# Moving the output stores from SyncE to ScalarE's DMA queue, one group of four images later

## What is computed

```
xa_n = inorm(xa)                                     # each image by its own mean and variance
k, q = spec_conv(xa_n, kw, (64, 64)), spec_conv(xa_n, qw, (64, 64))
v    = spec_conv(xa_n, vw, (256, 256))               # only 8 x 8 low frequencies are kept
att  = softmax(q @ k.T * sqrt(64 * 64)) @ v          # 64 x 64 among the images of a batch
att  = inorm(att) + xa
att_n = inorm(att)
mix  = spec_conv(att_n, mix_w, (256, 256)) + skip * att_n    # 32 x 32 frequencies
out  = inorm(inorm(mix)) + att
```

## Time and profile before

| what | value |
|---|---|
| median of three runs | 728.55 us (724.89 to 730.94) |
| the profiled execution | 727.67 us, its span 725.8 us |
| busy: TensorE, its weight loads | 662.7 us (91%), 591.5 us |
| busy: VectorE, ScalarE, GpSimd | 487.4, 331.3, 353.4 us |
| mean granted TensorE clock | 0.975 |
| DMA queue of SyncE | 71616 packets, 135.36 MB, 54.2% of 16 engines' time |
| three produce stages that also load | about 130 to 250, 298 to 418 and 469 to 589 us |
| last produce stage, stores only | about 641 to 726 us |

### The profile page before, as it was taken

One profiled execution on the slowest core, in us unless ns is written; L12 is line 12 of the kernel. 1 busy time (PEld: TensorE's weight loads), 2 busy tenths in 40 slices (PEclk: granted clock), 3 DMA queues, 4 the chain that ended last, 5 costly groups with the idle time before them and its releaser, 6 DMA issues.

```text
span 725.8 us, 15092 instructions
## 1 busy us (share of the span) xinstructions
PE 662.7 (91%) x5772; PEld 591.5 (81%) x5772; DVE 487.4 (67%) x1141; ACT 331.3 (46%) x710; POOL 353.4 (49%) x388
## 2 busy tenths in 40 slices
PE   6979898999999998999999999899999999886775
PEld 6979898788888898788888889878888889875653
DVE  3866658677777767577777766577777765765464
ACT  5768332464656413265566604246556532232121
POOL 0000013977970013895990003595994001398994
PEclk9999999999999999999999999999999999998698
DMA  8980000598889400399888700089888820035366
GB/s 272 389 328 2 1 1 1 206 318 279 286 302 304 165 1 1 115 305 310 287 284 305 254 1 2 1 289 323 286 280 300 285 95 2 1 135 214 116 229 235
DMA packets 71687, 136.32 MB, mean 188 GB/s; under 512 B 5376, under 2 KB 5888, under 8 KB 71616
## 3 DMA queue, kind: packets, MB, share of 16 engines
q1 hardware_dynamic: 71616, 135.36, 54.2%
HBM read 68.23 MB, written 67.11 MB: 186 GB/s over the span
## 4 chain that ended last, share of the span: by engine, by line
PE 63%; DVE 17%; POOL 9%; issue 3%; DMA 3%; ACT 2%; SPq 1%; DVEq 0%; ACTq 0%; POOLq 0%
PE psY L291 25%; PE psP L343 16%; POOL X L635 6%; PE psT L328 6%; PE psP L399 4%; PE psP L312 3%; PE psY L312 3%; DVE X L681 3%; DVE Y L681 3%; DVE QP L786 2%; DVE SQ L681 2%; DMA X<-in_x 2%; DMA out<-X 2%; ACT SQ L497 1%; POOL Y L618 1%
## 5 line engine op out<-in xcount | busy, mean ns | idle before, releaser
L635 POOL TENSOR_TENSOR X<-X,ALPHA 128x512 f32<-128x512 f32 x256 | 266.7, 1077 | 28.0 <-DVE IM L986 26.1
L291 PE MATMUL psY<-FWD,X 128*128 128x128 f32 x2048 | 249.7, 281 | 13.5 <-DMA X<-in_x 7.7
L291 PEld LDWEIGHTS psY<-FWD,X 128*128 128x128 f32 x2048 | 237.5, 194 | 28.7 <-issue 24.9
L681 DVE TENSOR_TENSOR X<-X,psP 128x512 f32<-128x512 f32 x256 | 165.4, 684 | 96.8 <-PE psP L343 87.0
L786 DVE TENSOR_REDUCE QP<-SQ 128x32 f32<-128x512 f32 x256 | 161.7, 679 | 60.5 <-ACT SQ L497 41.9
L343 PE MATMUL psP<-INVW,T 64*128 64x256 f32 x1024 | 151.2, 412 | 26.4 <-DVE X L681 18.8
L613 POOL TENSOR_TENSOR Y<-Y,OMEGA 128x256 f32<-128x256 f32 x32 | 25.6, 800 | 290.2 <-ACT Y L501 289.9
L497 ACT ACTIVATE SQ<-X 128x512 f32<-128x512 f32 x256 | 147.0, 622 | 24.1 <-DVE QP L786 11.5
L343 PEld LDWEIGHTS psP<-INVW,T 64*128 64x128 f32 x1024 | 98.4, 193 | 59.6 <-issue 36.7
L519 ACT ACTIVATE T<-psT,BIA,SCL 128x256 f32<-128x256 f32 x128 | 65.3, 561 | 128.1 <-PE psT L328 115.9
L489 ACT ACTIVATE Y<-psY 128x512 f32<-128x512 f32 x128 | 76.0, 594 | 66.5 <-PE psY L291 66.5
(11 more groups left out here) (168 smaller groups left out, 404.6 us busy)
## 6 DMA issues: line engine op xcount, KB each, us to landing
X<-in_x SPq DMA_DIRECT2D x128, 512.0 KB, 5.2
out<-X SPq DMA_DIRECT2D x128, 512.0 KB, 3.8
INVH<-t_inv_h SPq DMA_DIRECT2D x1, 256.0 KB, 4.9
LW<-in_low_w SPq DMA_DIRECT2D x1, 204.0 KB, 3.5
GWT<-t_w SPq DMA_DIRECT2D x1, 192.0 KB, 4.7
FWD<-t_fwd SPq DMA_DIRECT2D x1, 128.0 KB, 2.2
INVW<-t_inv_w SPq DMA_DIRECT2D x1, 128.0 KB, 4.7
LM<-in_low_mix SPq DMA_DIRECT2D x1, 68.0 KB, 3.2
```

The costliest lines, as they stand in the source:

```text
L291: last = mm(psY[p % 2][:, (2 * i + c) * 128:(2 * i + c + 1) * 128], X[:, 2 * p + i, a, c * 128:(c + 1) * 128], FWD[:, a, :], start=a == 0, ...
L635: P.tensor_tensor(v, v, al, MUL).then_inc(x_scaled, 1)
L681: return V.tensor_tensor(out, a, b, op)
```

## The change

SyncE's program loses the stores. It issues the loads of the next batch, each after the store of the same pair. ScalarE's program gains the 128 stores. For a batch that is followed by another, the stores of pairs 2(u-1) and 2(u-1)+1 stand in step u: in steps 1 and 2 both at the step's end, and in steps 3 to 16 one behind each of the two `keep_y`. In the last batch both stand at the end of the following step, and the last two pairs behind the loop. A store waits for the same count of `out_made` as before.

```diff
--- before.py
+++ after.py
@@ SyncE
-            def store(b, q):
-                sp.wait_ge(out_made, 64 * b + 2 * (q + 1))
-                sp.dma_start(out_v[b, :, 2 * q:2 * (q + 1), :],
-                             Xf[:, 2 * q:2 * (q + 1), :]).then_inc(store_done[q], 16)
             def batch(b, more):
-                for q in range(PAIRS + 1):
-                    if q < PAIRS:
-                        store(b, q)
-                    if more and q:
-                        sp.wait_ge(store_done[q - 1], 16 * b + 16)
-                        load(b + 1, q - 1)
+                for q in range(PAIRS if more else 0):
+                    sp.wait_ge(store_done[q], 16 * b + 16)
+                    load(b + 1, q)
@@ ScalarE
+            def store(b, q):
+                act.wait_ge(out_made, 64 * b + 2 * (q + 1))
+                nc.scalar.dma_start(out_v[b, :, 2 * q:2 * (q + 1), :],
+                                    Xf[:, 2 * q:2 * (q + 1), :]).then_inc(store_done[q], 16)
...
                             square(b + 1, 2 * p)
                             square(b + 1, 2 * p + 1)
                             keep_y(b + 1, p)
+                            if 2 * (u - 1) + p % 2 < PAIRS:
+                                store(b, 2 * (u - 1) + p % 2)
+                    elif u:
+                        store(b, 2 * u - 2)
+                        store(b, 2 * u - 1)
...
                 attend(b)
                 produce(b, b < B - 1)
+            store(B - 1, PAIRS - 2)
+            store(B - 1, PAIRS - 1)
```

## The result

The changed kernel takes 747.67 us (median of 4 runs, 739.64 to 753.89) against 728.6 us. The ratio is 1.023, with a 95% interval of 1.013 to 1.033. Timed again beside other kernels it took 747.96 us, ratio 1.027 (1.023 to 1.030). One of the four runs, 753.89 us, lay over 1.5% above the fastest and is not in the ratio. So it is 2.3 to 2.7% slower, 17 to 20 us; the forecast was 1.2%, 737 us, with a range of 728 to 746. The median lies just above that range; 728.6 us times the ratio, 745.3 us, lies just inside. The direction and the two places were right, their size was not. The profiled execution took 747.74 us, its span 745.7.

What follows compares the result with a forecast made beforehand. TensorE was taken to bound the kernel, with the last pair's HBM trip deciding at batch ends. Ends 7.8, clock 1.5 and starts 0.3 summed to 9.6 us on 727.67: 737.3 us, say 737, range 728 to 746.

Steps and rivals of the forecast that it cites:

- the two places: Ends and starts of the three produce stages, where later stores were to make TensorE wait: +7.8 and +0.3 us.
- What bounds the kernel, and where the change would bite: TensorE, busy 91%, sets the 7.02 us step; at batch ends the last pair's HBM trip sets or nearly sets it.
- The ends, 7.8 us and 1.5 for the clock: At three stage ends pair 31's store goes 2.7 us later: +7.8 us; TensorE pauses lower its clock: +1.5 us.
- The round trip itself I keep: At stage ends, pair 31's store and load were to take as long as before, only start later.
- "Nothing is added" for pairs 28 to 30: At stage ends, their forwards finish before pair 31 arrives: nothing added, but a TensorE pause of up to 3 us.
- The clock: At three ends, a pause before pair 30 may lower TensorE's granted clock: +1.5 us, from 0 to 5.1.
- The starts, 0.3 us: At three stage starts, stores of pairs 0 and 1 stand behind `mode_powers`, leaving no cover: 0.1 us each, +0.3.
- Steady steps, 0 with 2.3 us of cover: In the loop, a 9.0 us trip from medians fits the 11.3 us left after the later store: cost 0.
- one such miss at 1.1 us: In a steady step, if the cover went (7.2 + 5.2 = 12.4), TensorE would stand 1.1 us.
- ScalarE's issues, 0: In steady steps, two issues of 0.37 us delay the squares at most 0.48 us, under VectorE's 0.60 idle: 0.
- The rival of the dear issue: On ScalarE, issues of 0.8 us would add 12 us over 39 steps: 749 us; chance 0.13.
- Shorter trips: At the three ends, an own queue lets stores pass loads; 7.6 of 7.8 us return: 729 us; chance 0.27.

Runs made afterwards that it cites:

- early version: The changed kernel with all stores still on ScalarE's queue, but placed where the images are just finished; 731.01 us, ratio 1.003 against the kernel before.
- second profile: The changed kernel run again with no edit, profiled and timed beside other kernels; 747.96 us, ratio 1.027 against the kernel before.

## Why the prediction was half right

**What bounds the kernel, and where the change would bite**: right. The loss stands at the two places named, and the steady step kept its 7.02 us.

**The ends, 7.8 us and 1.5 for the clock**: the lateness was right. The store goes when `keep_y` starts, 2.4 us late at each end; alone, on one queue, that cost 6.6 us (last stores) and 7.9 us (all). In the changed kernel the ends lost 12.1 and 13.2. The step of the prediction that failed is "The round trip itself I keep: store and load of pairs 28 to 31 move later together, so the traffic around them stays alike". Around them were the loads of pairs 27 to 29, themselves late, and on a queue of its own a store takes longer beside them, 4.9 us in the median against 3.8. The trip of pair 31 went from 7.8, 8.7 and 9.5 to 9.1, 10.1 and 11.6 us at the three ends, 4.9 us together, and that is most of what the sum lacked there. "Nothing is added" for pairs 28 to 30 failed too. At the second end the load of pair 31 was in 0.6 us ahead, and what TensorE waited for was pair 29, 2.5 us. The early version puts 3.5 us on the queue alone.

**The clock**: about as put. In each of both profiles of the changed kernel the clock fell to half for 3.4 us at one of the three ends, the second; before, at none. That is at most 1.7 us of matmul time, where 1.5 stood in the sum. The second profile, at the second end (us, PE busy, granted clock, DMA share, GB/s):

```profile
428.00:432.00 4.00, 2.17 (x18) 1.00 0.81 266
432.00:434.00 2.00, 1.72 (x12) 0.80 0.51 192
434.00:436.00 2.00, 2.00 (x11) 0.50 0.00 0
436.00:438.00 2.00, 2.00 (x17) 0.85 0.00 0
438.00:440.00 2.00, 1.54 (x9) 1.00 0.00 0
```

**The starts, 0.3 us**: the term that was most mis-sized; 5.3 and 4.9 us. I took the landings of 3.1 and 3.9 us from a store and a load that stood alone, and looked at pairs 0 and 1 only. Now four stores go out within 4.5 us. The store of pair 0 goes when the sum had it, but its load takes 5.0 to 5.2 us instead of 3.9, and its forward stands 0.7 to 0.9 us later in each batch, 2.3 us of the 5.3. Pair 3 was not held back at all, since its store waited for `finish` before as well. But its trip went from 11.0 (478.88 to 489.85 us) to 13.6 us, in traffic that had been pushed together, and it adds another 2.3 us. In the second profile pair 0 has most of the loss, 3.2 of 4.9 us. Moved back to SyncE, the first four stores cost nothing.

**Steady steps, 0 with 2.3 us of cover**: the step's length was right, the cover was not enough. Since the store goes when `keep_y` starts, the room is 11.9 us and not 11.3. But the trip was put together from two medians over all pairs, 9.0 us. Whole trips before took 8.8 us in the median for even pairs from 8 to 26 and 10.9 for odd ones, so that an odd pair had 1 us of cover. In the changed kernel they take 9.3 and 11.2 us, and single trips reach 13.9 to 15.7. The cost varies from profile to profile, 0.8 and 5.9 us. I had priced one such miss at 1.1 us and put none into the sum.

**ScalarE's issues, 0**: right, with room. An issue took 0.38 us, at most 0.48, and held up no activation in the steady steps. The rival of the dear issue is out.

**Shorter trips** (the rival that would have ended at no change): wrong in sign, for the stores and for whole trips. The Trainium skill, "DMA: Bandwidth & Descriptors", section "Queues, rings and completion order", has each DMA engine take the queues with work in turn. By that rule a store on its own queue does not wait behind an earlier load, but a load issued a little later takes turns with it as well. The trace fits this: before, the store of an even pair was mostly issued 0.4 to 0.5 us ahead of a load (561.67 and 562.17 us for pair 26) and landed after 3.5 us in the median of pairs 8 to 26, that of an odd pair after 4.9; on ScalarE's queue both took 5.4, and 4.9 and 5.3 in the early version. In return the loads of even pairs landed after 3.8 us instead of 5.1. That the turns are the cause is argued, not shown; no run changed the order in which packets were served.

The same page's section "Issuing engines are not separate DMA queues" says that a second issuer only saves the time to issue. The early version bears it out as far as there is no gain: 0.3% slower.

## What to carry to other kernels

A transfer that is late by a little costs nothing until its trip passes the slack of the one consumer that is waiting, so compare slack with the longest whole trips under the new traffic, not with medians under the old. Work in place makes the store part of the next load's latency: issue it at once, or give the consumer one more step of lead. A second queue is no gain by itself: with the same times of issue the median store landed after 3.8 us on one queue and after 4.5 on two. And an experiment that moves an instruction between queues has to be checked for what then stands behind it.

## What was not expected of the hardware

- A DMA behind an activation in ScalarE's program was issued when that activation started, within 0.01 us, in 72 of the 84 stores that stand behind a `keep_y`. The other twelve, pairs 12 to 15 of each batch, went while an activation that stands before that `keep_y` was still running (179.42 us, 0.9 us ahead of its `keep_y`). In the steady steps the issue does not delay the next activation: 0.38 us of issue inside 0.60 us of `keep_y`.
- Four stores of 512 KB within 4.5 us, each followed by a load, took up to 6.6 and 7.2 us apiece, against at most 5.8 and 6.3 for the same four pairs before, when the stores were spread over 7.2 us.
- Without any change in the instructions ahead of them, steady steps of one program lost 0.8 us in one profile and 5.9 in another.
